# Graph layer with a segment maximum: the own message subtracted inside a TensorE accumulation, and four rank comparisons made one VectorE operation

## Chip, cores and metric

One core of one Trainium2 chip. The metric is the device time of one launch, in microseconds. The profile is of one such launch, and its times run from the first instruction.

## Reference

100,000 nodes with 128 values each; 25,000 random directed edges and one loop per node, all sorted by their target. Two layers follow each other, each on the layer-normed and rectified rows, each added back to its input. The change touches the first:

```python
row, col = edge_index[0], edge_index[1]          # source, target
h = relu(layernorm(x))
feat = concat([h[col], h[row] - h[col]], axis=-1)
messages = relu(feat @ W1 + b1) @ W2 + b2
out = segment_max(messages, col)                 # every node has its own loop
x = x + out
```

The second layer (mean of the neighbours' projections, then a gated unit) reads `relu(layernorm(x))` of this result. Nothing of it is changed.

## The kernel before

Since every node has a loop, each node's maximum starts from its own message, and only real edges can raise it. The first layer works through 261 groups of 384 nodes (three tiles of 128), with at most 128 real edges a group. For a group it

- loads a window of 512 sorted edge entries, four to a partition (`edges_in`), and compares the rank of each with the 128 slots of the group (`edge_slots`: `oneh`, four 128x128 comparisons). TensorE multiplies entries and comparisons (`sort`), which leaves the group's real edges in slots (`lst`) and, along the free axis, the marks where a new target begins (`reset`);
- computes row numbers (`row_numbers`), gathers the sources' and the targets' rows with two indirect DMAs on GpSimd (`gather`), and norms the three tiles and the two gathered ones (`statistics`, `averages`, `deviation`, `scales`, `shifts`, `normalize`); `shifts` writes `nm`, the product of mean and reciprocal deviation;
- turns the five (`turn_rows`, `columns`), runs the first matmul (`mlp`, `hidden`: five blocks of 128 columns, where block 3 is the target's own hidden row and block 4 the edge's), and the second for blocks 3 and 4 (`messages`, into PSUM `ps_m`);
- takes a running maximum over the edges of a target (`run_maximum`, a scan over columns with a reset at each new target), subtracts the target's own message (`gains`), turns that difference with TensorE (`turn_gains`) and rectifies it (`gains_turned`), so that each edge has a gain above the own message;
- adds b2, the own messages and the gains of each target's last edge in one PSUM accumulation (`results`), adds x (`add_x`), norms the result again (`statistics1`, `averages1`, `deviation1`, `scales1`, `shifts1`, `normalize1`: h1), and GpSimd adds both into `q_rows` (`carried`). Three arrays go to DRAM.

The five engines run these stages as a software pipeline. `fixed_loop` is given pairs (lag, stage); in iteration n an engine executes its stages in the order written, each for group n minus its lag. So each engine has a fixed order within an iteration, and the engines meet only through semaphores (`after`, `landed`). 24 iterations are peeled, then a hardware loop has 56 iterations to a turn. The orders that matter here:

```python
# VectorE
[(12, add_x), (8, scales), (8, shifts), (12, statistics1), (5, row_numbers), (12, averages1),
 (10, one_hot), (2, edge_slots), (12, scales1), (12, shifts1), (10, run_maximum), (7, statistics), (10, gains),
 (7, averages)]
# ScalarE
[(8, deviation), (11, gains_turned), (10, hidden), (4, sorted_edges), (9, columns), (12, deviation1), (8, normalize),
 (13, normalize1)]
# TensorE
[(9, turn_rows), (11, results), (10, messages), (3, sort), (9, mlp), (10, turn_gains)]
# GpSimd
[(6, gather), (13, carried)]
```

Of the kernel before, what the change touches and what calls it, by code (L numbers as in the profile page):

```python
# [8 lines left out]
P = 128  # L9
D = 128  # L10
TILES = 3
GROUP = TILES * P
UN = 8
# [7 lines left out]
F16 = mybir.dt.float16  # L21
BF16 = mybir.dt.bfloat16
I32 = mybir.dt.int32
ALU = mybir.AluOpType
# [57 lines left out]
def fixed_loop(eng, total, stages, span=UN):  # L82


    turns = (total - PEEL * UN) // span
    rest = total - PEEL * UN - turns * span
    for n in range(PEEL * UN):
        for lag, stage in stages:
            if n >= lag:
                stage(Step(0, n - lag, span))  # L90
    if turns > 0:
        with eng.Fori(0, turns) as i:
            for n in range(PEEL * UN, PEEL * UN + span):
                for lag, stage in stages:
                    stage(Step(i, n - lag, span))
    for n in range(rest + max(lag for lag, _ in stages)):
        for lag, stage in stages:
            if n - lag < rest:
                stage(Step(turns, PEEL * UN + n - lag, span))
# [1883 lines left out]
def layer_max_sorted(nc, env):  # L1983


    G, COLS, weights, lists = (env[k] for k in ("G", "COLS", "weights", "lists"))
    x, q_dram, h1_dram, edges_dram = (env[k] for k in ("x", "q_dram", "h1_dram", "edges_dram"))
    ident_f, other_i, first_edge, first_rank = (env[k] for k in ("ident_f", "other_i", "first_edge", "first_rank"))
    rows_dram = env["rows_dram"]
    SPREAD = 4  # L1990
    SPAN = 7 * UN
    WIDTH = 5 * P

    with ExitStack() as ctx:
        def sb(name, shape, dt=F32):
            return ctx.enter_context(nc.sbuf_tensor("m_" + name, shape, dt))

        def ps(name, cols=512):
# [4 lines left out]
        w2 = sb("w2", [P, D])  # L2003
# [5 lines left out]
        b2_wide = sb("b2_wide", [96, TILES, D], BF16)  # L2009
        ones_p = sb("ones_p", [96, P], BF16)  # L2010
        eps = sb("eps", [P, 1])
        iota_slot = sb("iota_slot", [P, P], F16)
        iota_loc = sb("iota_loc", [P, TILES, P], F16)
        base_f = sb("base_f", [P, G])

        win = sb("win", [P, UN, SPREAD, 4])
        oneh = sb("oneh", [P, 2, SPREAD, P], F16)
        lst = sb("lst", [P, UN, 4], F16)
        reset = sb("reset", [P, UN, P])
# [9 lines left out]
        hT = sb("hT", [P, 2, WIDTH])  # L2029
        hid = sb("hid", [P, 4, WIDTH])  # L2030
        runmax = sb("runmax", [P, 2, P])
        gain = sb("gain", [P, 2, P])
        gain_rows = sb("gain_rows", [P, 2, D])
        onehot = sb("onehot", [P, 2, GROUP])
        x1s = sb("x1s", [P, 4, GROUP])
# [9 lines left out]
        ps_h = ps("h", 1024)  # L2045
        ps_m, ps_g, ps_k, ps_x = (ps(q) for q in ("m", "g", "k", "x"))

        names = ("weights const prep oneh sorted srt idx bn mv std rs h tn hT hidep hide msge scan gain scT gT oh "
                 "xp x1 bn1 mv1 std1 rs1 h1 q go").split()
        like = dict(oneh="pe", xp="ext", gT="hi", q="O", list_out0="t1", list_out1="t2")  # L2050
        S = {q: env["named"](f"a_{like.get(q, q)}") for q in names}
        d_win, d_x, d_gat = ([env["named"](f"a_{q}{k}") for k in range(4)] for q in ("ent_in", "x_in", "gathered"))
        d_q, d_h1, d_lst = ([env["named"]("a_" + like.get(f"{q}{k}", f"{q}{k}")) for k in range(2)] for q in ("x1_out", "h1_out", "list_out"))
# [2 lines left out]
        def after(eng, name, st, per=1, back=0):  # L2056

            if st.past(back):
                eng.wait_ge(S[name], st.count(per, back))

        def landed(eng, sems, st, back=0, per=16):

            if st.past(back):
                eng.wait_ge(sems[st.slot(len(sems), back)], st.landed(len(sems), back, per))
# [44 lines left out]
        @block.gpsimd  # L2109
        def _(pool):  # L2110
            G_ = nc.gpsimd
            other = pool.value_load(other_i[0:1, 0:1], min_val=0, max_val=1)
            with pool.If(other < 1):
                G_.iota(iota_slot[:, :], pattern=[[1, P]], base=0, channel_multiplier=0, allow_small_or_imprecise_dtypes=True).then_inc(S["const"], 1)
                G_.iota(iota_loc[:, :, :], pattern=[[1, TILES], [TILES, P]], base=1, channel_multiplier=0,
                        allow_small_or_imprecise_dtypes=True).then_inc(S["const"], 1)
                G_.iota(base_f[:, :], pattern=[[GROUP, G]], base=-1, channel_multiplier=0,
                        allow_small_or_imprecise_dtypes=True).then_inc(S["const"], 1)
                G_.memset(eps[:, :], EPS).then_inc(S["const"], 1)
                G_.memset(ones_p[:, :], 1.0).then_inc(S["const"], 1)  # L2120

                def gather(st):
                    after(pool, "idx", st, per=2)
                    after(pool, "h", st, per=5, back=4)
                    pool.sem_inc(S["go"], 1)
                    for q in range(2):
                        G_.indirect_dma_start(out=xg[:, st.slot(4), q, :], out_offset=None, in_=x[:, :],  # L2127
                                              in_offset=bass.IndirectOffsetOnAxis(ap=idx[:, st.slot(4), q:q + 1], axis=0)
                                              ).then_inc(d_gat[st.slot(4)], 16)

                def carried(st):
                    after(pool, "x1", st)
                    after(pool, "h1", st, per=3)
                    landed(pool, d_q, st, back=4)
                    G_.tensor_tensor(q_rows[:, st.slot(4), :], x1s[:, st.slot(4), :], h1s[:, st.slot(4), :], ALU.add).then_inc(S["q"], 1)  # L2135

                fixed_loop(pool, G, [(6, gather), (13, carried)], SPAN)
# [62 lines left out]
        def _(pe):  # L2200
            T = nc.tensor
            other = pe.value_load(other_i[0:1, 0:1], min_val=0, max_val=1)
            with pe.If(other < 1):
                pe.wait_ge(S["weights"], 5 * 16)
                pe.wait_ge(S["const"], 5)
                pe.wait_ge(S["prep"], 7 + 3 * TILES)

                def sort(st):
                    after(pe, "oneh", st, per=4)
                    after(pe, "srt", st, per=2, back=1)  # L2210
                    words = win[:, st.slot(UN), :, :].rearrange("p c f -> p (c f)").bitcast(F16).rearrange("p (c f) -> p c f", c=SPREAD)
                    for c in range(SPREAD):
                        T.matmul(ps_k[:, 0:4], oneh[:, st.slot(2), c, :], words[:, c, 2:6], start=(c == 0), stop=(c == SPREAD - 1))
                    for c in range(SPREAD):
                        mm = T.matmul(ps_k[:, P:2 * P], words[:, c, 6:7].broadcast_to([P, P]), oneh[:, st.slot(2), c, :],  # L2215
                                      start=(c == 0), stop=(c == SPREAD - 1))
                    mm.then_inc(S["sorted"], 1)
# [15 lines left out]

                def messages(st):
                    after(pe, "hide", st)
                    after(pe, "gain", st, back=1)
                    T.matmul(ps_m[:, 0:2 * P], w2[:, :], hid[:, st.slot(4), 3 * P:WIDTH], start=True, stop=True).then_inc(S["msge"], 1)

                def turn_gains(st):
                    after(pe, "gain", st)  # L2240
                    after(pe, "gT", st, back=1)
                    T.transpose(ps_g[:, 0:D], gain[:, st.slot(2), :], ident_f[:, :]).then_inc(S["scT"], 1)  # L2242

                def results(st):
                    after(pe, "gT", st)
# [15 lines left out]
        def _(v):  # L2261
            V = nc.vector
            other = v.value_load(other_i[0:1, 0:1], min_val=0, max_val=1)
            with v.If(other < 1):
                done = [0]

                def link(ins):
                    done[0] += 1
                    ins.then_inc(S["prep"], 1)
                    v.wait_ge(S["prep"], done[0])  # L2270

                v.wait_ge(S["weights"], 5 * 16)
                v.wait_ge(S["const"], 5)
                link(V.tensor_tensor(w1d[:, :], w1a[:, :], w1b[:, :], ALU.subtract))
                link(V.memset(b2_wide[:, :, :], 0.0))
                link(V.tensor_copy(b2_part[:, 0, :], b2_row[:, :]))
                link(V.tensor_tensor(b2_rest[:, 0, :], b2_row[:, :], b2_part[:, 0, :], ALU.subtract))
# [6 lines left out]

                def edge_slots(st):
                    after(v, "sorted", st, back=2)
                    landed(v, d_win, st)
                    for c in range(SPREAD):
                        V.tensor_scalar(oneh[:, st.slot(2), c, :], iota_slot[:, :], first_rank[:, bass.ds(st.t, 1)], win[:, st.slot(UN), c, 0:1],  # L2289
                                        ALU.add, ALU.is_equal).then_inc(S["oneh"], 1)  # L2290

                def row_numbers(st):
                    after(v, "srt", st, per=2)
# [32 lines left out]

                def run_maximum(st):
                    after(v, "msge", st)
                    after(v, "gain", st, back=2)
                    V.tensor_tensor_scan(out=runmax[:, st.slot(2), :], data0=reset[:, st.slot(UN), :], data1=ps_m[:, P:2 * P],  # L2330
                                         initial=0.0, op0=ALU.add, op1=ALU.max).then_inc(S["scan"], 1)

                def gains(st):
                    after(v, "scan", st)
                    after(v, "scT", st, back=2)
                    V.tensor_tensor(gain[:, st.slot(2), :], runmax[:, st.slot(2), :], ps_m[:, 0:P], ALU.subtract).then_inc(S["gain"], 1)  # L2336

                def one_hot(st):
                    after(v, "xp", st, back=2)
# [27 lines left out]
                def shifts1(st):  # L2367
# [1 line left out]
                    V.scalar_tensor_tensor(out=nm1[:, st.slot(2), :], in0=mv1[:, st.slot(2), :, 0], scalar=-1.0, in1=rs1[:, st.slot(2), :],  # L2369
                                           op0=ALU.mult, op1=ALU.mult).then_inc(S["rs1"], 1)  # L2370

                fixed_loop(v, G, [(12, add_x), (8, scales), (8, shifts), (12, statistics1), (5, row_numbers), (12, averages1),
                                  (10, one_hot), (2, edge_slots), (12, scales1), (12, shifts1), (10, run_maximum), (7, statistics), (10, gains),
                                  (7, averages)], SPAN)


# [490 lines left out]
```

## Time and profile before

| | |
|---|---|
| median of 3 runs | 3772.24 us (3769.52 to 6292.41) |
| profiled execution, time | 3769.3 us |
| profiled execution, span | 3767.4 us |
| the first layer, first to last instruction | 570.5 to 2094.0 us |
| its pipeline, from the first output group to the last | 616 to 2093 us |
| busy over the whole span | PE 78%, DVE 88%, ACT 63%, POOL 58% |

PE is TensorE, DVE VectorE, ACT ScalarE, POOL GpSimd, SP SyncE, which issues most DMAs. A row of the timeline gives start, duration, engine, line, operation, what it writes and reads, and how many instructions are merged (xN); in brackets stands how long the engine had been idle and what released it. Instructions on VectorE overlap a little: the next often begins some 0.08 us before the one before it ends. Of the three runs one took 6292.41 us; the other two lie 2.7 us apart.

### The profile page before, as it was taken

How to read it: one execution, taken by the hardware profiler on the slowest of the kernel's cores; microseconds unless marked ns; L12 is line 12 of the kernel's file. 1: busy time of each engine (PE TensorE's matmuls, PEld its weight loads, DVE VectorE, ACT ScalarE, POOL GpSimd, SP SyncE). 2: the span in 40 equal slices, each digit the busy share in tenths (PEclk: the TensorE clock that was granted, in tenths of full speed). 3: DMA queues.
4: the chain of work that ended last, by engine and by line, in shares of the span. 5: the costliest groups of instructions: out<-in, count | busy, mean ns of one | idle time of the engine just before them, and what ended most of it. 6: DMA issues, size and time to landing. Idle time of an engine off the chain costs nothing. (4 is left out here: it accounts for less than half of the span.)

```text
span 3767.4 us, 92998 instructions
## 1 busy us (share of the span) xinstructions
PE 2934.9 (78%) x19557; PEld 1885.7 (50%) x19557; DVE 3300.9 (88%) x13396; ACT 2387.4 (63%) x5746; POOL 2186.0 (58%) x2359
## 2 busy tenths in 40 slices
PE   0144426888788788888888499999999999999998
PEld 0011105666666666666666255555555555555554
DVE  8844428999999999999999599999999999999998
ACT  0000007999899999989999266666666666666665
POOL 0166644555455445545554377777777777777774
PEclk9966658999999999999999699999999999999999
DMA  1000006776666666766766377777777777777775
GB/s 51 0 1 1 1 9 94 130 130 135 121 133 132 124 128 130 133 124 128 135 130 128 89 188 181 180 184 182 180 180 186 180 179 187 180 180 185 180 180 140
DMA packets 626188, 493.56 MB, mean 131 GB/s; under 512 B 330800, under 2 KB 599600, under 8 KB 625680
## 3 DMA queue, kind: packets, MB, share of 16 engines
q1 hardware_dynamic: 568016, 386.66, 41.2%
q0 software_dynamic: 57792, 102.97, 17.0%
q14 instruction: 280, 2.29, 0.4%
q8 instruction: 100, 1.64, 0.3%
HBM read 331.99 MB, written 157.29 MB: 130 GB/s over the span
## 5 line engine op out<-in xcount | busy, mean ns | idle before, releaser
L2543 POOL DMA_INDIRECT s_rows<-h_dram,s_idx x1044 | 992.3, 950 | 292.6 <-issue 244.4
L2135 POOL TENSOR_TENSOR m_q_rows<-m_x1s,m_h1s 128x384 f32<-128x384 f32 x261 | 260.6, 998 | 608.3 <-ACT m_h1s L2193 550.4
L2663 PE MATMUL sp_g<-s_wb,s_hT 128*128 128x512 f16 x2349 | 609.2, 379 | 0.0
L2676 PE MATMUL sp_g<-s_proj,s_onehot 128*128 128x384 f16 x3132 | 594.1, 326 | 0.0
L2127 POOL DMA_INDIRECT m_xg<-in_x_dram,m_idx x522 | 497.7, 954 | 155.8 <-issue 106.5
L2579 ACT ACTIVATE s_proj<-sp_p,s_share 128x384 f16<-128x384 f32 (+1 forms) x522 | 297.9, 571 | 229.6 <-PE sp_p L2651 228.8
L2651 PE MATMUL sp_p<-s_wq,s_dT 128*128 128x384 f16 x1566 | 344.7, 329 | 93.9 <-DVE s_proj L2787 92.8
L719 POOL DMA_INDIRECT lists_src<-p_ent,p_pos x240 | 233.6, 973 | 274.9 <-issue 212.3
L2676 PEld LDWEIGHTS sp_g<-s_proj,s_onehot 128*128 128x128 f16 x3132 | 306.3, 98 | 172.0
L2169 ACT ACT_TABLE_LOAD x1 | 1.3, 1283 | 577.7 <-PE mp_k L2215 577.7
L2590 ACT ACTIVATE s_ru<-sp_g,s_unscale 128x768 f32<-128x768 f32 x261 | 235.0, 900 | 190.1 <-PE sp_g L2676 190.1
L2157 ACT ACTIVATE m_h<-m_x,m_nm,m_rs 128x128 f32<-128x128 f32 x783 | 325.8, 479 | 1.2 <-DVE m_nm L2324 0.2
L2193 ACT ACTIVATE m_h1s<-m_x1s,m_nm,m_rs 128x128 f32<-128x128 f32 x783 | 325.5, 478 | 0.0
L2787 DVE SCALAR_TENSOR_TENSOR s_proj<-sp_p,s_share,s_proj 128x384 f16<-128x384 f32 (+1 forms) x522 | 316.5, 606 | 4.5 <-ACT s_proj L2579 4.5
L2663 PEld LDWEIGHTS sp_g<-s_wb,s_hT 128*128 128x128 f16 x2349 | 208.7, 98 | 158.4 <-issue 1.0
L2230 PE MATMUL mp_h<-m_hT,m_w1a 128*128 128x512 f32 x522 | 282.0, 622 | 0.0
L2594 ACT ACTIVATE sp_g<-s_pre,s_unscale 128x384 f32<-128x384 f32 x261 | 152.6, 585 | 202.8 <-DVE s_pre L2805 202.8
L2289 DVE TENSOR_SCALAR m_oneh<-m_iota_slot,first_rank,m_win 128x128 f16<-128x128 f16 x1044 | 272.2, 323 | 0.5 <-PE mp_k L2215 0.5
L2551 POOL TENSOR_TENSOR s_diff<-s_rows 128x256 f32<-128x256 f32 x261 | 191.4, 733 | 136.7 <-DVE s_split L2781 127.9
L2242 PE MATMUL mp_g<-ident_f,m_gain 128*128 128x128 f32 x261 | 85.6, 328 | 229.9 <-DVE m_gain L2336 229.0
L2651 PEld LDWEIGHTS sp_p<-s_wq,s_dT 128*128 128x128 f16 x1566 | 111.3, 98 | 275.5 <-DVE s_proj L2787 171.0
L743 PE MATMUL pp_rank<-p_B,before 128*128 128x261 bf16 x240 | 93.4, 389 | 187.9 <-DVE p_B L888 187.9
(270 smaller groups left out, 7886.0 us busy)
## 6 DMA issues: line engine op xcount, KB each, us to landing
m_x<-in_x_dram SPq DMA_DIRECT2D x261, 192.0 KB
h_dram<-m_h1s SPq DMA_DIRECT2D x261, 192.0 KB
q_dram<-m_q_rows SPq DMA_DIRECT2D x261, 192.0 KB
s_h_rows<-h_dram SPq DMA_DIRECT2D x261, 192.0 KB
s_q_rows<-q_dram SPq DMA_DIRECT2D x261, 192.0 KB, 4.7
out_dram<-s_out_rows SPq DMA_DIRECT2D x261, 192.0 KB
s_erow<-lists_dst SPq DMA_DIRECT2D x261, 128.0 KB
s_erow<-lists_src SPq DMA_DIRECT2D x261, 128.0 KB
```

Source lines behind the costliest of these rows:

```text
L2127: G_.indirect_dma_start(out=xg[:, st.slot(4), q, :], out_offset=None, in_=x[:, :], in_offset=bass.IndirectOffsetOnAxis(ap=idx[:, st.slot(4 ...
L2135: G_.tensor_tensor(q_rows[:, st.slot(4), :], x1s[:, st.slot(4), :], h1s[:, st.slot(4), :], ALU.add).then_inc(S["q"], 1)
L2157: A.activation(h[:, st.slot(2), q, :], rows, ACT.Identity, bias=nm[:, st.slot(4), q:q + 1], scale=rs[:, st.slot(4), q:q + 1]).then_inc(S[" ...
L2193: A.activation(h1s[:, st.slot(4), q * D:(q + 1) * D], x1s[:, st.slot(4), q * D:(q + 1) * D], ACT.Relu, bias=nm1[:, st.slot(2), q:q + 1], s ...
L2230: T.matmul(ps_h[:, 0:4 * P], w1a[:, :], hT[:, s2, 0:4 * P], start=True, stop=True)
L2289: V.tensor_scalar(oneh[:, st.slot(2), c, :], iota_slot[:, :], first_rank[:, bass.ds(st.t, 1)], win[:, st.slot(UN), c, 0:1], ALU.add, ALU.i ...
L2543: G_.indirect_dma_start(out=rows[:, s4, q, :], out_offset=None, in_=h1_dram[0:G * GROUP, :], in_offset=bass.IndirectOffsetOnAxis(ap=idx[:, ...
L2579: A.activation(proj[0:P - k, s2, k, 0, :], ps_p[0:P - k, 0:H3], ACT.Copy, scale=share[0:P - k, st.slot(4), k:k + 1]).then_inc(S["ph"], 1)
L2651: mm = T.matmul(ps_p[:, 0:H3], dT[:, s2, (2 * k + of) * P:(2 * k + of + 1) * P], wq[:, w, k, :], start=(q == 0), stop=(q == 2))
L2663: T.matmul(bank[:, t, :], hT[:, st.slot(4), of, t * P:(t + 1) * P], wb[:, w, :], start=(q == 0), stop=False, skip_group_check=True)
L2676: mm = T.matmul(ps_g[s2][:, t, 0:H3], onehot[:, st.slot(4), k, t * P:(t + 1) * P], proj[:, s2, k, w, :], start=False, stop=(k == 1 and w = ...
L2787: V.scalar_tensor_tensor(out=proj[0:P - k, s2, k, 1, :], in0=ps_p[0:P - k, 0:H3], scalar=share[0:P - k, st.slot(4), k:k + 1], in1=proj[0:P ...
```

## The change

The comparisons: before, each of four VectorE operations adds the group's first rank to a column of slot numbers and tests it against one of the four entries' ranks. Now a small stage `edge_ranks` subtracts the first rank from the group's four ranks per partition (128x4, into a new tile `slot`), and `edge_slots` makes all four comparisons in one operation on 128x512 elements, whose second input is `slot`, repeated along the columns. `iota_slot` is four times as wide. `edge_ranks` stands between `shifts` and `statistics1` in VectorE's order.

The own message: before, VectorE subtracts it from the running maximum (`gains`), and TensorE turns the difference. Now the stage `gains` is gone; TensorE multiplies the own hidden block with the negated W2 (`w2n`, made once), which gives the negated own message already turned, and adds the running maximum to it in the same accumulation by a multiplication with the identity. `messages` has only block 4 left, 128 columns in place of 256. Waits on `gain` become waits on `scan`, or on `scT`.

```diff
-        iota_slot = sb("iota_slot", [P, P], F16)
+        iota_slot = sb("iota_slot", [P, SPREAD, P], F16)
+        slot = sb("slot", [P, UN, SPREAD])
-        gain = sb("gain", [P, 2, P])
+        w2n = sb("w2n", [P, D])
...
-                G_.iota(iota_slot[:, :], pattern=[[1, P]], base=0, ...).then_inc(S["const"], 1)
+                G_.iota(iota_slot[:, :, :], pattern=[[0, SPREAD], [1, P]], base=0, ...).then_inc(S["const"], 1)
...
                 def sort(st):
-                    after(pe, "oneh", st, per=4)
+                    after(pe, "oneh", st)
...
                 def messages(st):
                     after(pe, "hide", st)
-                    after(pe, "gain", st, back=1)
-                    T.matmul(ps_m[:, 0:2 * P], w2[:, :], hid[:, st.slot(4), 3 * P:WIDTH], start=True, stop=True).then_inc(S["msge"], 1)
+                    after(pe, "scan", st, back=1)
+                    T.matmul(ps_m[:, 0:P], w2[:, :], hid[:, st.slot(4), 4 * P:WIDTH], start=True, stop=True).then_inc(S["msge"], 1)

                 def turn_gains(st):
-                    after(pe, "gain", st)
                     after(pe, "gT", st, back=1)
-                    T.transpose(ps_g[:, 0:D], gain[:, st.slot(2), :], ident_f[:, :]).then_inc(S["scT"], 1)
+                    T.matmul(ps_g[:, 0:D], hid[:, st.slot(4), 3 * P:4 * P], w2n[:, :], start=True, stop=False)
+                    after(pe, "scan", st)
+                    T.matmul(ps_g[:, 0:D], runmax[:, st.slot(2), :], ident_f[:, :], start=False, stop=True).then_inc(S["scT"], 1)
...
+                link(V.tensor_scalar(w2n[:, :], w2[:, :], -1.0, None, ALU.mult))
...
                 def edge_slots(st):
                     after(v, "sorted", st, back=2)
+                    after(v, "slot", st)
+                    V.tensor_tensor(oneh[:, st.slot(2), :, :], iota_slot[:, :, :],
+                                    slot[:, st.slot(UN), :].unsqueeze(2).broadcast_to([P, SPREAD, P]), ALU.is_equal).then_inc(S["oneh"], 1)
+
+                def edge_ranks(st):
                     landed(v, d_win, st)
-                    for c in range(SPREAD):
-                        V.tensor_scalar(oneh[:, st.slot(2), c, :], iota_slot[:, :], first_rank[:, bass.ds(st.t, 1)], win[:, st.slot(UN), c, 0:1],
-                                        ALU.add, ALU.is_equal).then_inc(S["oneh"], 1)
+                    V.tensor_scalar(slot[:, st.slot(UN), :], win[:, st.slot(UN), :, 0], first_rank[:, bass.ds(st.t, 1)], None,
+                                    ALU.subtract).then_inc(S["slot"], 1)
...
                 def run_maximum(st):
                     after(v, "msge", st)
-                    after(v, "gain", st, back=2)
-                    V.tensor_tensor_scan(out=runmax[:, st.slot(2), :], data0=reset[:, st.slot(UN), :], data1=ps_m[:, P:2 * P],
+                    after(v, "scT", st, back=2)
+                    V.tensor_tensor_scan(out=runmax[:, st.slot(2), :], data0=reset[:, st.slot(UN), :], data1=ps_m[:, 0:P],
                                          initial=0.0, op0=ALU.add, op1=ALU.max).then_inc(S["scan"], 1)
-
-                def gains(st):
-                    after(v, "scan", st)
-                    after(v, "scT", st, back=2)
-                    V.tensor_tensor(gain[:, st.slot(2), :], runmax[:, st.slot(2), :], ps_m[:, 0:P], ALU.subtract).then_inc(S["gain"], 1)
...
-                fixed_loop(v, G, [(12, add_x), (8, scales), (8, shifts), (12, statistics1), (5, row_numbers), (12, averages1),
-                                  (10, one_hot), (2, edge_slots), (12, scales1), (12, shifts1), (10, run_maximum), (7, statistics), (10, gains),
+                fixed_loop(v, G, [(12, add_x), (8, scales), (8, shifts), (2, edge_ranks), (12, statistics1), (5, row_numbers), (12, averages1),
+                                  (10, one_hot), (2, edge_slots), (12, scales1), (12, shifts1), (10, run_maximum), (7, statistics),
                                   (7, averages)], SPAN)
```

## Rows read from the trace of the kernel before

**Rows 1.** The page, busy time over the span and VectorE in 40 slices

```profile
PE 2934.9 (78%) x19557; PEld 1885.7 (50%) x19557; DVE 3300.9 (88%) x13396; ACT 2387.4 (63%) x5746; POOL 2186.0 (58%) x2359
...
DVE  8844428999999999999999599999999999999998
```

**Rows 2.** Busy time by engine in the stretch of the first layer's pipeline

```profile
616.00:2093.00 1477.00, 1212.78 (x8939) 943.58 (x8937) 1418.64 (x7652) 1370.29 (x3842) 741.93 (x766) 0.99 0.68 129
```

**Rows 3.** The timeline of one step, VectorE, ScalarE and GpSimd

```profile
1210.87 1.00 POOL L2135 TENSOR_TENSOR m_q_rows<-m_x1s,m_h1s 128x384 f32<-128x384 f32 x1 [2.32 <-ACT m_h1s L2193]
...
1211.30 0.59 DVE L2324 SCALAR_TENSOR_TENSOR m_nm<-m_mv,m_rs 128x5 f32<-128x5 f32 x1
...
1211.82 0.67 DVE L2353 BATCH_NORM_STATS2 m_stats<-m_x1s 128x6 f32<-128x128 f32 x3
...
1212.02 0.96 POOL L2127 DMA_INDIRECT m_xg<-in_x_dram,m_idx  x1
...
1212.40 0.19 DVE L2296 TENSOR_SCALAR m_idx<-m_lst 128x1 int32<-128x1 f16 x1
1212.52 0.20 DVE L2298 TENSOR_SCALAR m_idx<-m_lst,m_base_f 128x1 int32<-128x1 f16 x1
1212.66 0.31 DVE L2360 BATCH_NORM_AGGREGATE m_mv<-m_stats 128x2 f32<-128x6 f32 x3
...
1213.01 0.30 ACT L2186 ACTIVATE m_std<-m_mv,m_eps 128x3 f32<-128x3 f32 x1 [0.30 <-DVE m_mv L2360]
...
1213.20 1.05 DVE L2289 TENSOR_SCALAR m_oneh<-m_iota_slot,first_rank,m_win 128x128 f16<-128x128 f16 x4
...
1213.22 1.25 ACT L2157 ACTIVATE m_h<-m_x,m_nm,m_rs 128x128 f32<-128x128 f32 x3
...
1213.28 0.94 POOL L2127 DMA_INDIRECT m_xg<-in_x_dram,m_idx  x1 [0.30 <-issue]
...
1215.14 1.25 ACT L2193 ACTIVATE m_h1s<-m_x1s,m_nm,m_rs 128x128 f32<-128x128 f32 x3
...
1216.42 0.30 ACT L2150 ACTIVATE m_std<-m_mv,m_eps 128x5 f32<-128x5 f32 x1
...
1216.46 1.00 POOL L2135 TENSOR_TENSOR m_q_rows<-m_x1s,m_h1s 128x384 f32<-128x384 f32 x1 [2.24 <-ACT m_h1s L2193]
...
1216.75 0.19 DVE L2320 RECIPROCAL m_rs<-m_std 128x5 f32<-128x5 f32 x1
...
1216.97 0.51 DVE L2324 SCALAR_TENSOR_TENSOR m_nm<-m_mv,m_rs 128x5 f32<-128x5 f32 x1
```

**Rows 4.** Tile nm: durations in ns (min/median/max), first and last start

```profile
L2324 DVE SCALAR_TENSOR_TENSOR m_nm<-m_mv,m_rs x261: 164/518/871, 587.9 to 2073.8; 128x5 f32<-128x5 f32 x131
L2369 DVE SCALAR_TENSOR_TENSOR m_nm<-m_mv,m_rs x261: 160/163/165, 608.6 to 2090.8; 128x3 f32<-128x3 f32 x131
```

**Rows 5.** The timeline while the pipeline fills, before GpSimd's first addition

```profile
587.18 0.94 POOL L2127 DMA_INDIRECT m_xg<-in_x_dram,m_idx  x1 [0.30 <-issue]
...
587.92 0.17 DVE L2324 SCALAR_TENSOR_TENSOR m_nm<-m_mv,m_rs 128x5 f32<-128x5 f32 x1
```

**Rows 6.** ScalarE's waits, 616 to 2093 us: total us, times, longest us

```profile
ACT m_std L2186 <- DVE m_mv L2360: 74.0, 230, 3.8
```

**Rows 7.** VectorE's instructions by line and shape: busy us, mean ns, idle before

```profile
L2336 DVE TENSOR_TENSOR m_gain<-m_runmax,mp_m 128x128 f32<-128x128 f32 x261 | 70.5, 270 | 0.1
...
L2738 DVE TENSOR_TENSOR s_wq<-s_lhs,s_wq 128x768 f16<-128x768 f32 x1 | 1.0, 959 | 0.0
```

**Rows 8.** Tile s_split of the second layer: durations in ns

```profile
L2781 DVE TENSOR_TENSOR s_split<-s_diff,s_split x261: 410/414/543, 2144.5 to 3749.2; 128x256 f16<-128x256 f32 x131
```

**Rows 9.** TensorE's groups by line, 800 to 2000 us: busy us, mean ns, idle before

```profile
L2251 PE MATMUL mp_x<-m_w,m_hid 128*128 128x128 f32 x1248 | 174.8, 276 | 0.0
...
L2237 PE MATMUL mp_m<-m_hid,m_w 128*128 128x256 f32 x418 | 125.8, 383 | 0.0
...
L2242 PE MATMUL mp_g<-ident_f,m_gain 128*128 128x128 f32 x209 | 68.6, 328 | 188.3 <-DVE m_gain L2336 188.3
```

More of the change, by code:

```diff
@@ L2046, in layer_max_sorted @@
         ps_m, ps_g, ps_k, ps_x = (ps(q) for q in ("m", "g", "k", "x"))
-        names = ("weights const prep oneh sorted srt idx bn mv std rs h tn hT hidep hide msge scan gain scT gT oh "
+        names = ("weights const prep slot oneh sorted srt idx bn mv std rs h tn hT hidep hide msge scan scT gT oh "
                  "xp x1 bn1 mv1 std1 rs1 h1 q go").split()
-        like = dict(oneh="pe", xp="ext", gT="hi", q="O", list_out0="t1", list_out1="t2")
+        like = dict(slot="dp", oneh="pe", xp="ext", gT="hi", q="O", list_out0="t1", list_out1="t2")
         S = {q: env["named"](f"a_{like.get(q, q)}") for q in names}
@@ L2113, in _ @@
             with pool.If(other < 1):
-                G_.iota(iota_slot[:, :], pattern=[[1, P]], base=0, channel_multiplier=0, allow_small_or_imprecise_dtypes=True).then_inc(S["const"], 1)
+                G_.iota(iota_slot[:, :, :], pattern=[[0, SPREAD], [1, P]], base=0, channel_multiplier=0, allow_small_or_imprecise_dtypes=True).then_inc(S["const"], 1)
                 G_.iota(iota_loc[:, :, :], pattern=[[1, TILES], [TILES, P]], base=1, channel_multiplier=0,
@@ L2205, in _ @@
                 pe.wait_ge(S["const"], 5)
-                pe.wait_ge(S["prep"], 7 + 3 * TILES)
+                pe.wait_ge(S["prep"], 8 + 3 * TILES)
                 def sort(st):
-                    after(pe, "oneh", st, per=4)
+                    after(pe, "oneh", st)
                     after(pe, "srt", st, per=2, back=1)
```

## The prediction

> **What bounds the kernel now.** I read the busy table and the slices first: VectorE is at nine tenths or more from the seventh slice to the twenty-second, which is the first layer [rows 1]. Taken alone that says that every VectorE instruction removed is time gained. The window over the pipeline says much the same: in 1477 us VectorE is busy 1418.6 us, ScalarE 1370.3, TensorE 1212.8, GpSimd 741.9, at a granted clock of 0.99 [rows 2]. Per step (260 of them) that is 5.68 us, of which VectorE 5.46, ScalarE 5.27, TensorE 4.66. ScalarE is so close to VectorE that at most 107 us (1477 less 1370) could be gained before it is the bound itself.
>
> Then I read one step in the timeline, asking of each instruction what it waits for, and here the first reading breaks. The small product nm (L2324, 128x5) takes 0.59 us at 1211.30 and 0.51 us at 1216.97. It ends at 1211.89 and 1217.48; GpSimd's addition ends at 1211.87 and 1217.46 [rows 3]. I followed this through the stretch: in 240 of 248 steps nm ends 0.02 us behind the addition. Over all groups nm takes 164 ns at the least and 518 in the median, while its sister of 128x3 elements, which never meets the addition, takes 160 to 165 [rows 4]; and in the fill, before any addition has run, nm itself takes 0.17 us, with a gather of GpSimd running beside it [rows 5]. So about 0.35 us of what counts as busy VectorE time in each step is a wait for GpSimd's addition, and the addition's end is what sets VectorE's next work.
>
> The chain that sets the step is then this, all from [rows 3]. The addition runs 1210.87 to 1211.87. nm ends, statistics1 starts at 1211.82, row numbers at 1212.40 and 1212.52, averages1 ends at 1212.97. ScalarE, idle for 0.30 us on just that, starts its deviation at 1213.01, runs normalize from 1213.22 and normalize1 from 1215.14 to 1216.39 without a gap, and that end lets the next addition go at 1216.46. Sum: 1.00 - 0.05 + 1.15 + 0.04 + 0.21 + 1.92 + 1.25 + 0.07 = 5.59 us, which is the distance of the two additions. The waits agree: ScalarE waits 230 times, 74 us in all, for averages1 [rows 6]. VectorE's half of the step between averages1 and nm (one hot, comparisons, scan, statistics, gains, averages, add x) isn't in this chain. Nor can nm escape the addition by coming earlier: it needs the deviation that ScalarE starts behind normalize1 (1216.42), then the reciprocal (1216.75), and so is issued at 1216.97 at the earliest, half a microsecond into an addition that started at 1216.46.
>
> On the nm stall the Trainium skill has a rule (SBUF — State Buffer, section "Who interferes with whom"): a VectorE instruction with two SBUF inputs contends with a GpSimd instruction that reads SBUF, and whichever starts first holds the shared ports to its end. The trace agrees, with nm ending 0.02 us behind the addition.
>
> **The change, part by part.**
>
> *Comparisons.* Removed: four operations, 1.05 us together [rows 3]. Added: one tensor-by-tensor operation on 128x512. No row has its shape; the nearest has mixed f32 and f16 inputs on 128x768 elements and takes 959 ns [rows 7], and f32 minus f16 on 128x256 takes 414 [rows 8]. The slope is 545 ns for 512 elements, so 512 elements take about 414 + 545/2 = 0.69 us. Saved: some 0.36 us of VectorE a step, all of it between averages1 and nm, that is off the chain. Its value is nothing; it makes VectorE arrive early at the reciprocal, which waits for ScalarE's deviation.
>
> *Gains.* Removed: 270 ns a step [rows 7], in the same half. Also nothing.
>
> *Ranks.* Added: a 128x4 operation with a pointer scalar, between nm and statistics1. This is the one edit on the chain. nm ends as before with the addition; the ranks follow; statistics1, both row numbers, averages1, and so ScalarE's deviation, normalize, normalize1 and the next addition are all queued behind them. The nearest rows are the row numbers, also one element wide or so with a scalar from memory: start to start 0.12 us (1212.40 to 1212.52) and 0.14 us (to 1212.66) [rows 3]. I take 0.12. Upper bound: a quarter of the four comparisons, which have 128 columns and two pointers, 0.26 us. Lower bound: zero, if the time hides in the hand-over from nm. Its wait for the edge window is moved some 1.3 us forward in VectorE's order, but the window was issued more than two steps earlier and VectorE never idles for it before the comparisons, so that wait is free. The ranks run in the iterations from 2 to 262; the chain stands from iteration 14, so 249 steps pay: 249 x 0.12 = 30 us; bounds 0 and 65 us.
>
> *TensorE.* Messages of half the width, a 128x128 product in place of a 128x256 one; one 128x128 product more; the turning, one pass before, becomes an ordinary product of two passes. From the busy time of the groups, a product of two passes on 128 columns costs 2 x 174.8/1248 = 0.28 us, the old message 2 x 125.8/418 = 0.60, the old turning 0.33 [rows 9]. New less old: 3 x 0.28 - 0.60 - 0.33 = -0.09 us, and at worst, with 0.33 for each product, +0.06. TensorE has 1.0 us free a step [rows 2], 0.9 of it (188.3 us in 209 steps) just before the turning, waiting for the gain [rows 9]. It now waits for the scan, which ends earlier by the five statistics and the gain. Behind that wait stands turn_rows, which needs normalize anyway, and it comes sooner. Nothing on the chain moves, since ScalarE reads the turned gains only behind its deviation.
>
> *Once.* The wider iota and the negated W2 stand ahead of the first comparison. Bounds: nothing, and one GpSimd addition on 384 columns plus a small VectorE operation, 1.00 + 0.26 = 1.3 us. I take 1 us.
>
> **The new comparison and GpSimd.** It has two SBUF inputs, the four old ones had one tensor each, and it runs beside the gathers (1212.02 to 1214.22 in this step [rows 3]). In the second layer an operation with two SBUF inputs runs between gathers, 44 of 261 times over one, and takes 410 to 543 ns, never a gather's 0.95 us more [rows 8]; nm in the fill took 0.17 us with a gather running [rows 5]. So I cost it at nothing. Were it held to the end of the second gather, it would lose up to 0.9 us. VectorE's spare time after the change is about 0.36 + 0.27 + the 0.35 of nm's wait = 0.98 us, so even then the step would hardly grow.
> The page named above speaks against this edit by the same rule, since a second SBUF input is what makes an operation contend; it adds that descriptor making needs the write side, by which the gathers leave it alone. By the strict rule the sum would be at most the rival below; by the row it stays.
>
> **Sum.** 3769.3 (the profiled execution's own time, span 3767.4) + 30 + 1 = 3800 us. Its own time is 2.9 us below the median of the runs, so I say 3801. That is +0.8%; a measurement of this kernel can tell about 2% from no change, so I call it no change.
>
> **Rivals.**
> 1. *VectorE's instructions are the bound and nm's length is its own.* For it: 96% busy in the stretch. Then the step falls by 0.36 + 0.27 - 0.12 = 0.51 us until ScalarE is the bound, which gives 107 us less at most, some 20 us of it being stalls at the turns of the hardware loop that stay: 3682 us, -2.3%. Against it: nm's end tied to the addition in 240 steps, and ScalarE's 230 waits. Chance 6%.
> 2. *The ranks, in front of the chain, queue for GpSimd's gather as nm does for the addition.* The gather starts 0.15 us behind the addition (1212.02 against 1211.87), the ranks would start about 0.1 us before that; if the gather gets in first, each step pays its 0.95 us: 249 x 0.95 = 237 us, 4037 us. It decides as soon as the ranks start later than the gather. Against it: nm in the fill started inside a gather and wasn't held [rows 5]. Chance 4%.
> 3. *The comparison is held by the gathers and VectorE's spare time isn't enough*, by another 0.05 to 0.1 us a step: 3813 to 3826 us. Chance 6%, inside my range.
> 4. *The ranks hide wholly and VectorE's earliness evens out late steps*: 8 of 248 steps ended their nm late, 20 us in all. 3752 to 3772 us. Chance 10%.
>
> The forecast (0.08 to 0.26 us for the ranks, 3789 to 3835) has 71%, and what is left, 3%, is for a lateness that I don't see, on the slow side. Range 3766 to 3835: it leaves out rivals 1 and 2, the lower part of 4 and the unseen. Faster by over 2%: rival 1, 6%. Slower by over 2%: rival 2 and the unseen, 7%. Within: 87%.
>
> **What the profile after will show.** nm still ends 0.02 us behind the addition, median near 520 to 600 ns. A new idle time of VectorE before the reciprocal L2320's counterpart, released by ScalarE's deviation, of about 0.5 us a step, so VectorE's share falls while the step doesn't. The ranks begin just before nm ends; statistics1 starts 0.12 us later behind nm than before. ScalarE's idle time before deviation1 grows from 0.30 to about 0.42 us. The new comparison takes near 0.69 us, TensorE's turning waits less. The distance of two additions goes from 5.59 to 5.71. Wrong would make it: nm's duration falling to 0.17, an operation that takes over a gather's length, or an idle time of ScalarE other than that before deviation1.

## The result, and the profile after

The changed kernel takes 3793.59 us in the median of five runs (3789.25 to 3797.73), the kernel before 3772.24 us on the same chip (3768.32 to 3774.54; one run of 6292.41 us, which the comparison leaves out). The ratio is 1.0056, 95% interval 1.0045 to 1.0068: slower by 21 us, where 29 were forecast against the median. The profiled execution took 3797.73 us, 28 us above that of before, for which the sum said 31.

First the page, busy time over the span and VectorE in 40 slices, to be held against [rows 1], and the window over the pipeline, against [rows 2].

```profile
PE 2960.7 (78%) x20340; PEld 1948.3 (51%) x20340; DVE 3266.9 (86%) x12614; ACT 2360.0 (62%) x5746; POOL 2198.9 (58%) x2359
...
DVE  8844428999899999989999589999999999999998
```

```profile
616.00:2115.00 1499.00, 1239.97 (x9720) 1007.49 (x9719) 1382.64 (x6898) 1340.82 (x3839) 747.99 (x764) 0.99 0.64 127
```

VectorE has 782 instructions fewer and is busy for less time in a longer stretch. Its digits are still nearly all nines, so the slices alone would have told nothing.

The timeline of one step, VectorE, ScalarE and GpSimd, against [rows 3]:

```profile
1211.94 1.00 POOL L2136 TENSOR_TENSOR m_q_rows<-m_x1s,m_h1s 128x384 f32<-128x384 f32 x1 [2.45 <-ACT m_h1s L2194]
...
1212.23 0.74 DVE L2331 SCALAR_TENSOR_TENSOR m_nm<-m_mv,m_rs 128x5 f32<-128x5 f32 x1
...
1212.89 0.22 DVE L2296 TENSOR_SCALAR m_slot<-m_win,first_rank 128x4 f32<-128x4 f32 x1
...
1213.02 0.67 DVE L2355 BATCH_NORM_STATS2 m_stats<-m_x1s 128x6 f32<-128x128 f32 x3
...
1213.87 0.31 DVE L2362 BATCH_NORM_AGGREGATE m_mv<-m_stats 128x2 f32<-128x6 f32 x3
...
1214.21 0.30 ACT L2187 ACTIVATE m_std<-m_mv,m_eps 128x3 f32<-128x3 f32 x1 [0.60 <-DVE m_mv L2362]
...
1214.40 0.68 DVE L2291 TENSOR_TENSOR m_oneh<-m_iota_slot,m_slot 128x512 f16<-128x512 f16 x1
...
1215.00 0.17 DVE L2367 RECIPROCAL m_rs<-m_std 128x3 f32<-128x3 f32 x1
...
1216.34 1.25 ACT L2194 ACTIVATE m_h1s<-m_x1s,m_nm,m_rs 128x128 f32<-128x128 f32 x3
...
1216.84 0.45 DVE L2322 BATCH_NORM_AGGREGATE m_mv<-m_stats 128x2 f32<-128x6 f32 x5 [0.18 <-DVE m_stats L2315]
...
1217.67 1.00 POOL L2136 TENSOR_TENSOR m_q_rows<-m_x1s,m_h1s 128x384 f32<-128x384 f32 x1 [0.78 <-ACT m_h1s L2194]
```

nm ends at 1212.97, the addition at 1212.94. Behind nm stands the new operation, and statistics1 starts 0.05 us after nm's end, where before it started 0.07 us ahead of that end. The additions are 5.73 us apart in this step; the median over all steps went from 5.66 to 5.79 us. ScalarE's waits for averages1, against [rows 6], and nm's durations, against [rows 4]:

```profile
ACT m_std L2187 <- DVE m_mv L2362: 138.6, 251, 1.6
```

```profile
L2331 DVE SCALAR_TENSOR_TENSOR m_nm<-m_mv,m_rs x261: 164/656/1012, 589.3 to 2101.1; 128x5 f32<-128x5 f32 x131
```

What VectorE saved came back as a longer nm (median 656 ns for 518) and as two stretches of idle time on VectorE, which the part on its spare time below adds up. ScalarE waits longer for averages1.

### The profile page after: what moved, and what is told of

The parts are those of the page before. It is cut to its first block and busy times, and to the rows that moved or that the text cites. A ratio compares the mean times of both kernels' runs of the same rounds, so it can differ in the third digit from the quotient of the medians.

```text
span 3795.7 us, 93323 instructions
## 1 busy us (share of the span) xinstructions
PE 2960.7 (78%) x20340; PEld 1948.3 (51%) x20340; DVE 3266.9 (86%) x12614; ACT 2360.0 (62%) x5746; POOL 2198.9 (58%) x2359
## 5 line engine op out<-in xcount | busy, mean ns | idle before, releaser
L2128 POOL DMA_INDIRECT m_xg<-in_x_dram,m_idx x522 | 505.8, 969 | 154.7 <-issue 100.6
L2224 PE MATMUL mp_t<-ident_f,m_h 128*128 128x128 f32 x1305 | 200.8, 285 | 67.5 <-ACT m_h L2158 51.6
L2250 PE MATMUL mp_x<-m_b_wide,m_ones_p 96*128 96x384 bf16 x261 | 88.0, 337 | 194.4 <-ACT m_gain_rows L2182 189.7
```

## Experiments

Eleven kernels, each timed against the kernel before on its own chip. The median of the kernel before lies between 3768 and 3788 us, by chip and session, so ratios are compared. "Step" is the median distance of two of GpSimd's additions in the trace; 5.66 us before, 5.79 changed.

**1. The ranks off the chain.** In the changed kernel:

```diff
-[(12, add_x), (8, scales), (8, shifts), (2, edge_ranks), (12, statistics1), (5, row_numbers), (12, averages1),
+[(12, add_x), (8, scales), (8, shifts), (12, statistics1), (5, row_numbers), (12, averages1), (2, edge_ranks),
```

> The changed kernel with edge_ranks moved from in front of statistics1 to behind averages1 in VectorE's order. Theory (the chain addition, nm, statistics1, row numbers, averages1, ScalarE, next addition sets the step): the ranks leave the chain, the step falls from 5.79 to 5.66 us, and the time is that of the kernel before within 5 us, 3767 to 3778 us. Rival (VectorE's own throughput sets the step, the order within it is indifferent): no difference from the changed kernel, 3790 to 3797 us. Rival (the 21 us come from TensorE's extra product): no difference either.

Ratio 0.9988 (0.9976 to 1.0001), step 5.67 us. The same instructions in another order: the whole cost of the change is gone. Against the changed kernel's 1.0056 that is 0.7%, about 26 us. Neither TensorE's extra product nor VectorE's throughput can do that.

**2. Only the gains.** The changed kernel with the four old comparisons and no `edge_ranks`:

```diff
-V.tensor_tensor(oneh[...], iota_slot[:, :, :], slot[...].broadcast_to([P, SPREAD, P]), ALU.is_equal)
+for c in range(SPREAD):
+    V.tensor_scalar(oneh[..., c, :], iota_slot[:, :], first_rank[...], win[..., c, 0:1], ALU.add, ALU.is_equal)
```

> Only the second part of the change: the own message subtracted in TensorE, the four old comparisons kept. Theory: VectorE loses 0.27 us a step off the chain, which is worth nothing: 3767 to 3777 us. Rival (VectorE's throughput): 0.27 x 261 = 70 us less, 3700 us. Rival (TensorE's extra product is what costs): 3790 us or more.

Ratio 0.9989 (0.9975 to 1.0004), step 5.67 us: a quarter of a microsecond of VectorE work removed from every step is worth nothing that the interval can tell.

**3. Only the comparison.** The kernel before with `edge_ranks` and the one comparison, `gains` kept:

```diff
-[(12, add_x), (8, scales), (8, shifts), (12, statistics1), ...
+[(12, add_x), (8, scales), (8, shifts), (2, edge_ranks), (12, statistics1), ...
```

> Only the first part of the change: ranks and one comparison, the old gains kept. Theory: the whole cost is here, 0.13 us in each of 249 steps less what late steps give back: 3790 to 3803 us; perhaps more, since VectorE then has 0.27 us less to spare. Rival (TensorE): as before, 3772 us. Rival (VectorE's throughput): 0.30 - 0.13 = 0.17 us a step less, 3728 us.

Ratio 1.0037 (1.0024 to 1.0051), 14 us, step 5.81 us. The cost is in this half. The time in microseconds fell into the expected band only because that chip was slower altogether; by the ratio 14 us is somewhat under the expected 18 to 31. Against runs 1 and 2 on the same chip (3784 us both) it is 18 to 19 us longer, with a step longer by 0.13 us.

**4. nm late, in the kernel before.** Nothing of the change; one stage moved past three:

```diff
-[(12, add_x), (8, scales), (8, shifts), (12, statistics1), (5, row_numbers), (12, averages1),
+[(12, add_x), (8, scales), (12, statistics1), (5, row_numbers), (12, averages1), (8, shifts),
```

> The kernel before with one stage moved: shifts (nm) behind averages1, so that GpSimd's addition is over when nm comes, and statistics1, row numbers and averages1 run beside it. Theory: nm falls from 0.52 to 0.17 us, the chain is cut at GpSimd, and the step falls until VectorE's own work (5.66 - 0.35 = 5.31 us) or ScalarE's (5.27 us) bounds it: 0.30 to 0.35 us in 249 steps, 3685 to 3698 us. Rival (nm's length is its own, VectorE's throughput is the bound): no change, 3772 us. Rival (nm comes too late for normalize now): slower, up to 0.2 us a step, 3820 us.

Ratio 0.9889 (0.9867 to 0.991), 42 us less, half of what was expected. The tile nm:

```profile
L2324 DVE SCALAR_TENSOR_TENSOR m_nm<-m_mv,m_rs x261: 128/132/177, 588.5 to 2063.7; 128x5 f32<-128x5 f32 x131
```

The same instruction on the same data takes 132 ns when it comes after the addition: its length before was waiting. The step fell to 5.36 us as expected, but the mean only to 5.63. VectorE's waits in the stretch say why:

```profile
DVE m_stats L2308 <- DMA m_xg<-in_x_dram,m_idx: 52.9, 39, 3.7
DVE m_runmax L2330 <- PE mp_m L2237: 22.6, 30, 1.7
DVE m_stats L2308 <- DMA m_x<-in_x_dram: 13.1, 9, 4.4
```

With shorter steps the gathered rows are sometimes late; 65 steps lay over 0.3 us above the median, 13 in the kernel before.

**5. nm late, in the changed kernel.** The same move, with the ranks behind nm:

```diff
-[(12, add_x), (8, scales), (8, shifts), (2, edge_ranks), (12, statistics1), (5, row_numbers), (12, averages1),
+[(12, add_x), (8, scales), (12, statistics1), (5, row_numbers), (12, averages1), (8, shifts), (2, edge_ranks),
```

> The changed kernel with shifts (nm) moved behind averages1, and edge_ranks behind it. In the old kernel the same move took the median step from 5.66 to 5.36 us and the time down by 1.1%, with late gathers and late TensorE taking the rest. Theory: VectorE's savings (0.30 and 0.27 us a step) were worthless only while the addition held nm; with nm late they count until ScalarE's 5.27 us bound: median step 5.27 to 5.30 us, 15 to 25 us below the old kernel with the same move, ratio to the kernel before 0.982 to 0.986. Rival (the savings never count, since gathers set the pace by now): ratio 0.989, as the old kernel with the move.

Ratio 0.9823 (0.9806 to 0.9839), step 5.19 us. The intervals of this and of run 4 don't meet, though the two were taken on different chips. So the same change, its ranks now behind nm, that costs 0.56% in one order of VectorE's stages gains some 0.7% in the other, where nothing holds nm.

**6. The addition split.** In the changed kernel:

```diff
-G_.tensor_tensor(q_rows[..., :], x1s[..., :], h1s[..., :], ALU.add).then_inc(S["q"], 1)
+G_.tensor_tensor(q_rows[..., 0:D], x1s[..., 0:D], h1s[..., 0:D], ALU.add)
+G_.tensor_tensor(q_rows[..., D:GROUP], x1s[..., D:GROUP], h1s[..., D:GROUP], ALU.add).then_inc(S["q"], 1)
```

> The changed kernel, with GpSimd's addition into q_rows split in two instructions, the first third of the columns and then the rest. Theory (GpSimd's instruction holds nm to its own end, and nm gets in between two): nm ends about 0.5 us after normalize1's end in place of 1.2, the chain shortens by 0.4 to 0.5 us, the median step falls to about 5.4 us: ratio to the kernel before 0.975 to 0.990, late gathers included. Rival (GpSimd keeps VectorE out over both instructions, which together take 1.2 us): the step grows by 0.2 us, ratio 1.015 to 1.02. Rival (nm's length has nothing to do with the addition): as the changed kernel, 1.0056.

Ratio 1.007 (1.0056 to 1.0084), step 5.79 us. The time is near the last rival's 1.0056, but its reason is wrong, for nm did get shorter. The timeline:

```profile
1212.80 0.45 POOL L2136 TENSOR_TENSOR m_q_rows<-m_x1s,m_h1s 128x128 f32<-128x128 f32 x1 [1.86 <-ACT m_h1s L2195]
...
1213.08 0.20 DVE L2332 SCALAR_TENSOR_TENSOR m_nm<-m_mv,m_rs 128x5 f32<-128x5 f32 x1
1213.20 0.77 DVE L2297 TENSOR_SCALAR m_slot<-m_win,first_rank 128x4 f32<-128x4 f32 x1
1213.21 0.73 POOL L2137 TENSOR_TENSOR m_q_rows<-m_x1s,m_h1s 128x256 f32<-128x256 f32 x1
...
1213.88 0.67 DVE L2356 BATCH_NORM_STATS2 m_stats<-m_x1s 128x6 f32<-128x128 f32 x3
```

nm did slip in between (0.20 us). But now the ranks, one tensor of four elements, took 0.77 us and ended at 1213.97, with the second addition (1213.94). The hold had passed to the next instruction that can be held.

**7. A shorter addition.** In the changed kernel, two of three tiles added. It leaves out the third tile of `q_rows`, which stays zero, so its result is not that of the reference:

```diff
-G_.tensor_tensor(q_rows[..., :], x1s[..., :], h1s[..., :], ALU.add)
+G_.tensor_tensor(q_rows[..., 0:2 * D], x1s[..., 0:2 * D], h1s[..., 0:2 * D], ALU.add)
...
+G_.memset(q_rows[:, :, :], 0.0)
```

The last line stands ahead of the loop, once, 1.4 us.

> The changed kernel, with GpSimd's addition done for two of the three tiles only; the third tile of q is left out. Theory: the addition takes 0.73 us in place of 1.00 (as the second layer's addition on 256 columns does), nm ends 0.27 us earlier, still 0.02 us behind the addition, and the median step falls by the same 0.27 us to 5.52; 249 steps, 66 us less, part of it lost to late gathers: ratio to the kernel before 0.988 to 0.993. Rival (GpSimd, 50% busy, isn't in the chain): no change from 1.0056.

Ratio 0.9905 (0.989 to 0.992), step 5.54 us. The addition and nm:

```profile
L2137 POOL TENSOR_TENSOR m_q_rows<-m_x1s,m_h1s x261: 721/724/732, 619.6 to 2079.2; 128x256 f32<-128x256 f32 x131
```

```profile
L2332 DVE SCALAR_TENSOR_TENSOR m_nm<-m_mv,m_rs x261: 164/381/477, 589.6 to 2060.3; 128x5 f32<-128x5 f32 x131
```

The addition lost 0.275 us (999 to 724 ns), nm 0.275 (656 to 381), the step 0.26 (5.79 to 5.54). An engine that is busy for half the stretch (748 of 1499 us in the changed kernel) stands fully in the chain.

**8. Gathers with a step more to land.** Run 5, and in all five engines each stage from the statistics of the gathered rows on has its lag raised by one:

```diff
-[(6, gather), (13, carried)]
+[(6, gather), (14, carried)]
...
-(10, one_hot), (2, edge_slots), (12, scales1), (12, shifts1), (10, run_maximum), (7, statistics), (7, averages)
+(11, one_hot), (2, edge_slots), (13, scales1), (13, shifts1), (11, run_maximum), (8, statistics), (8, averages)
```

> As the run with nm late in the changed kernel, and every stage from the statistics of the gathered rows on one iteration later in all five engines, so that a gather has a whole step more to land; the amount of work is the same but for one iteration more to fill the pipeline. Theory (with the addition out of the chain, landings of gathers set the late steps): VectorE's waits for gathered rows, 53 us in the old kernel with nm late, fall below 5 us; a further 30 to 60 us less than the run without it, ratio to the kernel before 0.967 to 0.977. Rival (late landings are only a symptom of a transfer queue that is full): the waits move to other transfers and the time stays within 10 us of the run without it.

Ratio 0.9699 (0.9675 to 0.9723), the fastest of all, 113 us less than the kernel before. Waits of VectorE for gathered rows no longer appear among its longest. The window over most of the pipeline:

```profile
616.00:1960.00 1344.00, 1175.71 (x9673) 991.43 (x9672) 1238.78 (x6873) 1312.85 (x3826) 766.52 (x761) 0.99 0.79 141
```

ScalarE is busy 1312.9 of 1344 us, 98%, and so is the likely next bound. No run here tests that, and a busy share alone misled about VectorE.

**9. nm late, the ranks left where the change put them.** This tests what run 6 brought up:

```diff
-[(12, add_x), (8, scales), (8, shifts), (2, edge_ranks), (12, statistics1), (5, row_numbers), (12, averages1),
+[(12, add_x), (8, scales), (2, edge_ranks), (12, statistics1), (5, row_numbers), (12, averages1), (8, shifts),
```

> The changed kernel with shifts (nm) moved behind averages1, but edge_ranks left in front of statistics1. In the run with the addition split, nm was free at 0.17 us and edge_ranks, a one-input operation on 128x4, took 0.68 us and ended with the second addition. Theory (GpSimd's addition holds edge_ranks too; behind nm that was only hidden): edge_ranks now takes the hold, 0.7 us or so, ends 0.03 us behind the addition, and the chain stands as in the kernel before: step 5.65 us, ratio 1.000, 0.997 to 1.003. Rival (only operations with two SBUF tensors are held, and the ranks were late for another reason): as the run with both moved, 0.982.

Ratio 1.0019 (1.0004 to 1.0034), step 5.67 us. The tiles slot and nm, and one step:

```profile
L2296 DVE TENSOR_SCALAR m_slot<-m_win,first_rank x261: 188/759/861, 575.5 to 2061.2; 128x4 f32<-128x4 f32 x131
```

```profile
L2331 DVE SCALAR_TENSOR_TENSOR m_nm<-m_mv,m_rs x261: 128/131/159, 587.6 to 2096.0; 128x5 f32<-128x5 f32 x131
```

```profile
1213.23 1.00 POOL L2136 TENSOR_TENSOR m_q_rows<-m_x1s,m_h1s 128x384 f32<-128x384 f32 x1 [0.64 <-ACT m_h1s L2194]
...
1213.49 0.77 DVE L2296 TENSOR_SCALAR m_slot<-m_win,first_rank 128x4 f32<-128x4 f32 x1
```

The ranks end at 1214.26, the addition at 1214.23. In run 1 they come behind averages1, and 234 of the 261 start while a gather is running; the same instruction takes 198 ns in the median:

```profile
L2296 DVE TENSOR_SCALAR m_slot<-m_win,first_rank x261: 194/198/434, 575.8 to 2059.1; 128x4 f32<-128x4 f32 x131
```

**10. The addition split and the ranks behind averages1.** Runs 1 and 6 together:

```diff
-(8, shifts), (2, edge_ranks), (12, statistics1), (5, row_numbers), (12, averages1),
+(8, shifts), (12, statistics1), (5, row_numbers), (12, averages1), (2, edge_ranks),
...
-G_.tensor_tensor(q_rows[..., :], x1s[..., :], h1s[..., :], ALU.add).then_inc(S["q"], 1)
+G_.tensor_tensor(q_rows[..., 0:D], x1s[..., 0:D], h1s[..., 0:D], ALU.add)
+G_.tensor_tensor(q_rows[..., D:GROUP], x1s[..., D:GROUP], h1s[..., D:GROUP], ALU.add).then_inc(S["q"], 1)
```

> The changed kernel with the addition split in a third and two thirds, and edge_ranks behind averages1; nm stays in its old place. Theory: nm slips in between the two additions, 0.55 us earlier than now, and nothing in front of averages1 is held by the second, since statistics and row numbers never were; the step falls to ScalarE's bound of about 5.2 us: ratio 0.979 to 0.986. Rival (splitting never helps): 1.000, as the changed kernel with the ranks moved alone.

Ratio 0.9928 (0.9907 to 0.9949), outside the expected band. nm takes 193 ns in the median (651 in run 1), and the step is 5.32 us. But 122 steps lie over 0.3 us above that, and they have two causes. In 79 of them nm starts 0.41 us or more after the start of the first addition, when the second one has begun, and ends with the second:

```profile
1202.69 0.45 POOL L2136 TENSOR_TENSOR m_q_rows<-m_x1s,m_h1s 128x128 f32<-128x128 f32 x1 [2.16 <-ACT m_h1s L2195]
...
1203.10 0.73 POOL L2137 TENSOR_TENSOR m_q_rows<-m_x1s,m_h1s 128x256 f32<-128x256 f32 x1
1203.10 0.74 DVE L2332 SCALAR_TENSOR_TENSOR m_nm<-m_mv,m_rs 128x5 f32<-128x5 f32 x1
...
1208.51 0.45 POOL L2136 TENSOR_TENSOR m_q_rows<-m_x1s,m_h1s 128x128 f32<-128x128 f32 x1 [2.32 <-ACT m_h1s L2195]
```

These steps take 5.82 us in the median and make up 40 of the 128 us by which the 122 exceed the median. Where nm starts 0.37 us behind the start of the first addition it isn't held (165 ns in the median of 52 steps). So the split opens a gap that nm can miss by 0.05 us; the expectation counted on it in every step. In the other 43, which make up the remaining 88 us, nm is not held by the second addition; there VectorE's waits are the likely cause, 58.4 us for gathered rows and 12.6 for TensorE's messages. Against run 1 (0.9988) the split is worth 0.6%, where run 6 alone made it look useless.

**11. The two moves without the change.** The kernel before, with nm late and the lags of run 8:

```diff
-[(12, add_x), (8, scales), (8, shifts), (12, statistics1), (5, row_numbers), (12, averages1),
+[(13, add_x), (9, scales), (13, statistics1), (5, row_numbers), (13, averages1), (9, shifts),
...
-(10, run_maximum), (7, statistics), (10, gains), (7, averages)
+(11, run_maximum), (8, statistics), (11, gains), (8, averages)
```

> The kernel before with nm behind averages1 and every stage from the statistics of the gathered rows on one iteration later: the same two moves as in the fastest run, without the change itself. Theory: with the addition out of the chain and the gathers early, VectorE's 5.3 us bound the old kernel and ScalarE's 5.1 to 5.2 us the changed one, so the change is worth 0.15 to 0.2 us in each of 261 steps, 40 to 50 us: ratio to the kernel before 0.979 to 0.984, against 0.970 with the change. Rival (the change is worth nothing in any setting): 0.970.

Ratio 0.9738 (0.9712 to 0.9764), step 5.26 us against 5.18 in run 8. With both moves the change is worth 0.4%, less than was expected (the two runs are from different chips), and the two intervals overlap by a little; that it helps here is likely and not settled. I had put VectorE's bound of the old kernel at 5.3 us and it runs at 5.26.

## Why the prediction was right, point by point

*The bound.* Right. The chain through GpSimd's addition, nm, averages1 and ScalarE is shown three ways: an instruction taken off it gives its time back (run 1), shortening the addition shortens the step by as much (run 7), and taking nm out of the addition's way opens the step to 5.36 and 5.19 us (runs 4 and 5). nm ended within 0.06 us of the addition in 237 of 248 steps after the change, 240 before.

*Comparisons and gains worth nothing.* Right (run 2; and run 3 is no faster than before). The comparison took 684 ns, 0.69 forecast. But its saving counted from start to start is 0.30 us, not 0.36: before, the comparisons start at 1213.20 [rows 3] and the next instruction, a reciprocal, at 1214.10; now it is 1214.40 to 1215.00. I had used durations, 1.05 and 0.69 us, and the next instruction starts 0.15 us before four comparisons end, but only 0.08 before one does.

*Ranks.* The term was 0.12 us a step; the median step grew by 0.137 us (5.655 to 5.792), from start to start of ranks and statistics1 0.13. That is 34 us over 249 steps, where the profiled executions lie 28 us apart, the medians of the five runs 21, and run 1 and the changed kernel 26 by their ratios. The forecast of 3801 was 7 us high. Late steps account for the difference between the two traces: by the starts of all 261 additions, 13 steps before lie over 0.3 us above the median, by 22.8 us in all, and 10 after, by 14.4 us; 34 - 8 = 26 us. Whether the change makes late steps rarer isn't shown. Each trace is one execution, and runs 1 and 2, with about the old step, have 28 and 21 such steps, worth 37 and 31 us. So rival 4, that late steps even out, stays open as a part of the result; its other half, that the ranks hide wholly, is wrong.

*TensorE.* Right that it doesn't matter. Its busy time grew from 82.1% of the stretch to 82.7%, which at mean steps of 5.68 and 5.78 us is 4.66 and 4.78 us a step: 0.12 us more, above my bounds of -0.09 to +0.06, and none of it in the chain. The price of a product was too low: I took 0.28 us from a group of six in a row, 0.33 at worst, and the three new ones, of two passes each, take 0.39 (80.5 us in 206 steps), 0.39 (79.3 in 205) and 0.40 us (82.7 in 205).

*The new comparison and GpSimd.* Right: 673 to 697 ns over all 261 groups, of which 233 start while a gather is running. It is never held by them.

*VectorE's spare time.* Wrong in shape. I expected 0.5 us idle before the reciprocal, released by ScalarE; a wait there shows 16 times, 5.6 us in all. These rows say where the saved time went, first before, then after:

```profile
1215.29 0.47 DVE L2308 BATCH_NORM_STATS2 m_stats<-m_xg 128x6 f32<-128x128 f32 x2
...
1215.94 0.45 DVE L2315 BATCH_NORM_AGGREGATE m_mv<-m_stats 128x2 f32<-128x6 f32 x5
...
1216.30 0.52 DVE L2346 TENSOR_TENSOR m_x1s<-m_x,mp_x 128x384 f32<-128x384 f32 x1
```

```profile
1216.19 0.47 DVE L2315 BATCH_NORM_STATS2 m_stats<-m_xg 128x6 f32<-128x128 f32 x2
...
1217.20 0.52 DVE L2348 TENSOR_TENSOR m_x1s<-m_x,mp_x 128x384 f32<-128x384 f32 x1
...
1217.49 0.29 ACT L2151 ACTIVATE m_std<-m_mv,m_eps 128x5 f32<-128x5 f32 x1
...
1217.81 0.19 DVE L2327 RECIPROCAL m_rs<-m_std 128x5 f32<-128x5 f32 x1
```

The averages (L2322 after) start 0.65 us behind the statistics of the gathered rows both before (1215.29 to 1215.94) and after (1216.19 to 1216.84). They wait for the statistics right in front of them, and `gains` had stood in between and covered that: removing 0.27 us of work uncovered 0.18 us of waiting (44.9 us in 248 steps), and VectorE comes no earlier for it. The 0.30 us of the comparisons do make it earlier, and they split in two. The reciprocal still starts 0.03 us behind ScalarE's deviation, so 0.16 us of them pass in front of it: it starts 0.09 us after the end of add_x, where before it started 0.07 us ahead of that end, and idle time so short isn't listed among the waits. The other 0.14 us are nm, which is issued that much earlier in its addition and held that much longer. None of this had a price in the sum, so the forecast didn't suffer from it.

*ScalarE's wait* before deviation1 grew to 0.55 us a time (138.6/251), not 0.42. The step grew by 0.14 us only, and the rest is ScalarE's own busy time, which fell from 5.27 to 5.17 us a step; why its instructions are a little shorter wasn't followed.

*Rival 2,* that the ranks are held, named the right victim and the wrong holder. Gathers don't hold them (run 1, 234 starts within one). The addition does (runs 6 and 9), but in the changed kernel nm stands in front and takes the hold for them. It cost nothing here; it takes the whole gain of moving nm, as run 9 shows against run 5.

On this the Trainium skill (SBUF — State Buffer, section "Who interferes with whom") names a second way to contend, besides two SBUF inputs: a tensor-scalar operation from SBUF to SBUF can enter a mode that takes both ports. Runs 6 and 9 agree that a one-tensor operation can be held, 0.68 and 0.76 us in the median against 0.20; that such a mode is why no run here shows.

## What to carry to other kernels

An engine at 96% may be waiting inside its instructions: compare the same instruction's shortest and median duration, and look whose end its end follows, before counting busy time as work. Here an operation saved off the chain was worth nothing, and a small one put on it cost 0.13 us, its time from start to start, in every step, so the first question of an added stage is where in the order it stands. And when a hold is removed from one instruction, the next one that can be held inherits it: move both, then look at what is late next, here the gathers. The kernel before gained 2.6% by such moves (run 11), and 3.0% with the change (run 8).

## What the runs showed of the hardware

GpSimd's addition of two f32 tensors in SBUF held two kinds of VectorE instruction to 0.02 or 0.03 us behind its own end: a product of two SBUF tensors of five elements (132 to 167 ns when free, 518 to 656 in the median), and a subtraction with one SBUF tensor of four elements and a pointer scalar (198 ns free, 759 held). It did not hold the reciprocal of 128x5 (189 ns, inside the addition in [rows 3]), nor, in run 4, the batch-norm statistics of one tensor that then ran beside it (0.68 us for three from 1214.92, beside an addition from 1214.55 to 1215.55; 0.67 without one in [rows 3]). The hold goes by the instruction: between two additions back to back a waiting VectorE instruction gets in and ends 0.02 us behind the first (run 6), and one that starts when the second has begun is held to the end of that (79 steps of run 10).

The product nm takes 132 ns behind averages1 and 164 to 167 behind the reciprocal whose result it reads. Why, no run here tells.
